# Four preactivation convolution layers on one core: load semaphore split four ways, streamed read issued from ScalarE, VectorE program written out over the images

## The reference

```python
# layer 0: y = leaky(einsum('bchw,oc->bohw', x, W2) + b), slope 0.1
#          (y - min) / (max - min + 1e-8), min and max per image and channel
# layer 1: rfft2, a complex 3x3 convolution over the spectrum, + bias, irfft2
# layer 2: x quantized by the largest |x| of the WHOLE batch, int8 3x3 conv, scale, bias
# layer 3: circular 3x3 convolution (written with FFTs in the reference)
x = x + _L0_conv_ref(_gn(x), ...)
x = x + _L1_conv_ref(_gn(x), ...)
x = x + _L2_conv_ref(_gn(x), ...)
x = x + _L3_conv_ref(_gn(x), ...)
```

## Time and profile before

| | |
|---|---|
| median of 3 runs | 7022.31 us (7016.27 to 7039.35) |
| the profiled execution | 7036.58 us, its span 7033.7 us |
| busy in the span | TensorE 82%, VectorE 71%, ScalarE 64%, GpSimd 39% |
| mean granted TensorE clock | 0.942 |
| DMA | 959.36 MB, mean 136 GB/s |
| issued from SP | 42.4% of the 16 DMA engines' span |
| issued from ScalarE | 6.2% |
| phase 1 | up to 4900 us |
| streamed reads | 224 of 512 KB |
| loads into X in phase 1 from the input | 448 of 256 KB |

### The profile page before, as it was taken

One profiled execution on the slowest core, in us unless ns is written; L12 is line 12 of the kernel. 1 busy time (PEld: TensorE's weight loads), 2 busy tenths in 40 slices (PEclk: granted clock), 3 DMA queues, 4 the chain that ended last, 5 costly groups with the idle time before them and its releaser, 6 DMA issues. The chain is left out here.

```text
span 7033.7 us, 203784 instructions
## 1 busy us (share of the span) xinstructions
PE 5742.6 (82%) x64138; PEld 3678.9 (52%) x64138; DVE 5000.3 (71%) x9849; ACT 4504.5 (64%) x8680; POOL 2727.5 (39%) x4633
## 2 busy tenths in 40 slices
PE   0259968968987896996897898897698898899889
PEld 0037747746764773774675676675243343343334
DVE  7857776767777776776776787787776676676674
ACT  0367656647656665665664654654887778778776
POOL 2145545536545554554553654654011111111112
PEclk9979989989998998998998999998899999999999
DMA  6315524542551551453354154254476676676665
GB/s 179 114 48 164 166 79 121 165 128 74 167 156 48 158 166 58 144 167 103 99 163 145 51 142 125 56 143 113 87 205 169 168 197 167 169 193 180 167 181 132
DMA packets 535643, 959.36 MB, mean 136 GB/s; under 512 B 121946, under 2 KB 126682, under 8 KB 532826
## 3 DMA queue, kind: packets, MB, share of 16 engines
q1 hardware_dynamic: 471898, 815.99, 42.4%
q10 hardware_dynamic: 63104, 134.23, 6.2%
HBM read 560.66 MB, written 287.60 MB: 121 GB/s over the span
## 5 line engine op out<-in xcount | busy, mean ns | idle before, releaser
L868 PE MATMUL pM<-gw,xh 64*128 64x256 f16 (+1 forms) x24960 | 1153.4, 247 | 205.3 <-DMA back<-c_back 205.0
L1570 PE MATMUL pC<-xs,taps 128*128 128x512 f16 x4608 | 1093.8, 382 | 106.4 <-DMA xhalo<-xs 101.3
L868 PEld LDWEIGHTS pM<-gw,xh 64*128 64x128 f16 x24960 | 981.7, 96 | 352.9 <-DMA back<-c_back 230.7
L604 POOL TENSOR_TENSOR X<-X,zo 128x256 f32 (+1 forms) x512 | 370.9, 724 | 1494.5 <-DVE X L1015 1494.5
L1570 PEld LDWEIGHTS pC<-xs,taps 128*128 128x128 f16 x4608 | 448.6, 98 | 669.5 <-DVE xs L1619 90.2
L1466 POOL TENSOR_TENSOR xn<-xn,one_col 128x1 f32<-128x1 f32 x520 | 170.7, 328 | 1402.0 <-ACT xn L1500 1402.0
L775 PE MATMUL pM<-X,mix0s 64*64 64x512 f32 x2304 | 529.9, 632 | 183.9 <-DVE X L987 108.7
L589 POOL TENSOR_TENSOR X<-X,rl 128x512 f32 x384 | 478.0, 1274 | 517.3 <-ACT rl L635 517.0
L1486 ACT ACTIVATE scaled<-X,qbias,qscale 128x512 f32 (+1 forms) x512 | 411.1, 804 | 356.3 <-DMA X<-after_layer 289.4
L1015 DVE SCALAR_TENSOR_TENSOR X<-pZ,X 128x512 f32 (+1 forms) x512 | 353.9, 691 | 376.2 <-ACT zo L664 374.4
L1508 ACT ACTIVATE xs<-xn 128x1028 f16<-128x1028 f32 x520 | 545.7, 1049 | 88.3 <-POOL xn L1467 87.3
(11 more groups left out here) (236 smaller groups left out, 13835.1 us busy)
## 6 DMA issues: line engine op xcount, KB each, us to landing
gw<-row_weights SPq DMA_DIRECT2D x520, 288.0 KB, 3.6
after_layer<-X SPq DMA_DIRECT2D x512, 256.0 KB
out_dram<-result SPq DMA_DIRECT2D x512, 256.0 KB
stage<-in_x_dram SPq DMA_DIRECT2D x224, 512.0 KB
X<-in_x_dram SPq DMA_DIRECT2D x448, 256.0 KB
X<-after_layer ACTq DMA_DIRECT2D x224, 512.0 KB, 5.8
xhalo<-xs SPq DMA_DIRECT2D x504, 96.4 KB, 3.6
qhalo<-q SPq DMA_DIRECT2D x496, 96.2 KB, 4.0
```

What stands on the lines that cost most here:

```text
L604: nc.gpsimd.tensor_tensor(X[:, j, 0], X[:, j, 0], zo[:, k], ALU.add)
L868: nc.tensor.matmul(pY[:, r, col:col + nd * P], row(xh, r)[:, k, p, ri, off:off + P], weights(r, q_, d, nd, ri), start=ri == 0 and off == 1 ...
L1570: nc.tensor.matmul(bank, taps3[:, d, wh], xs[:, h, own, d:d + W], start=d == 0 and n == 0, stop=False)
```

## The change

The single semaphore `loaded` becomes four, one for each tile number modulo 4; `stream` moves from SP's program to ScalarE's; VectorE's loop over the images is unrolled in the program text.

```diff
-            loaded = sem("loaded", p1)
+            loaded_0 = sem("loaded_0", p1)
+            loaded = [sem(f"loaded{k}", p1) for k in range(4)]
...
                     def load(b, j, k, n, more):
-                        wait_alone(sp, loaded, (b * J + j) * 16, passed)
+                        wait_alone(sp, loaded[k], (b * (J // 4) + n) * 16, passed)
...
-                            sp.dma_start(Xf[:, j], image_view(b)[:, :, j]).then_inc(loaded, 16)
+                            sp.dma_start(Xf[:, j], image_view(b)[:, :, j]).then_inc(loaded[k], 16)
...
-                    def turn(b, n, k, g, more, last):
-                        if not last and k % 2 == 0 and (4 <= n < J if isinstance(n, int) else True):
-                            stream(b + 2, g * 2 + k // 2, k // 2)
+                    def turn(b, n, k, g, more):
...
                         for u in range(4):
                             row_weights(b, u, u)
-                        if not last:
-                            for p in range(2):
-                                stream(b + 2, p, p)
...
-                    for p in range(2):
-                        stream(1, p, p, True)
-                    with sp.Fori(1, J // 4) as g:
-                        for s in range(2):
-                            stream(1, g * 2 + s, s)
...
                 def _(act):
+                    def stream(b, p, s, first=False):
+                        if not first:
+                            wait_alone(act, sum_x_done, (b - 1) * PAIRS + p, passed)
+                        act.dma_start(stage[:, s].rearrange("p (t w) -> p t w", t=2),
+                                     image_view(b)[:, :, bass.ds(2 * p, 2)]).then_inc(staged[s], 16)
...
-                    def step(b, i, k4, on, more=False, g=None):
+                    def step(b, i, k4, on, more=False, g=None, ahead=False):
                         k, o = k4 % 2, (k4 + 1) % 2
+                        if ahead and k == 0:
+                            stream(b + 2, i // 2 - 2 if isinstance(i, int) else g * 2 + k4 // 2 - 2, k4 // 2)
                         if on(4):
                             odd_out(b, i - 4, k)
...
-                    with act.Fori(0, J // 4) as g:
+                    for p in range(2):
+                        stream(1, p, p, True)
+                    with act.Fori(0, J // 4 - 1) as g:
                         for s in range(2):
                             next_squares(0, g * 2 + s, s, g)
                             next_sums(0, g * 2 + s, s)
+                            stream(1, g * 2 + s + 2, s)
+                    for p in range(PAIRS - 2, PAIRS):
+                        next_squares(0, p, p % 2, J // 4 - 1)
+                        next_sums(0, p, p % 2)
...
                     def next_pair(b, p):
-                        wait_alone(pe, loaded, ((b + 1) * J + 2 * p + 2) * 16, passed)
+                        for t in range(2):
+                            wait_alone(pe, loaded[(2 * p + t) % 4], ((b + 1) * (J // 4) + p // 2 + 1) * 16, passed)
...
-                    with dve.Fori(0, B) as b:
+                    for b in range(B):
```

More of the change, by code:

```diff
@@ L297, in _ @@
                             if c:
[L298 to L302, removed]
+                                act.wait_ge(loaded_0, 16 * c)
+                            act.dma_start(Xf[:, 4 * c:4 * c + 4], image_view(0)[:, :, 4 * c:4 * c + 4]).then_inc(loaded_0, 16)
+                        act.wait_ge(loaded_0, 16 * (J // 4))
+                        for k in range(4):
+                            act.sem_inc(loaded[k], 16 * (J // 4))
                     @block.vector
@@ L524, in load @@
                         if more:
[L525 removed]
+                            sp.dma_start(Xf[:, j], image_view(b)[:, :, j]).then_inc(loaded[k], 16)
                         else:
[L528 to L535, removed]
[L537 to L540 removed]
+                            sp.dma_start(Xf[:, j], x2s[0].rearrange("(j s) c w -> (s c) j w", s=BANDS)[:, j]).then_inc(loaded[k], 16)
+                    def turn(b, n, k, g, more):
                         if not isinstance(n, int) or n + 4 <= J:
@@ L546, in turn, with image @@
                             load(b + 1, n - 4, k, g - 1, more)
-                    def image(b, more, last):
+                    def image(b, more):
                         for u in range(4):
                             row_weights(b, u, u)
-                        if not last:
-                            for p in range(2):
-                                stream(b + 2, p, p)
                         for n in range(4):
-                            turn(b, n, n, 0, more, last)
+                            turn(b, n, n, 0, more)
                         with sp.Fori(1, J // 4 - 1) as g:
                             for k in range(4):
-                                turn(b, g * 4 + k, k, g, more, last)
+                                turn(b, g * 4 + k, k, g, more)
                         for n in range(J - 4, J + 4):
-                            turn(b, n, n % 4, n // 4, more, last)
-                    for p in range(2):
-                        stream(1, p, p, True)
-                    with sp.Fori(1, J // 4) as g:
-                        for s in range(2):
-                            stream(1, g * 2 + s, s)
+                            turn(b, n, n % 4, n // 4, more)
                     if B > 2:
                         with sp.Fori(0, B - 2) as b:
-                            image(b, True, False)
+                            image(b, True)
                     if B > 1:
-                        image(B - 2, True, True)
-                    image(B - 1, False, True)
+                        image(B - 2, True)
+                    image(B - 1, False)
                     for k in range(4):
                         sp.wait_ge(stored[k], 16 * (B * J // 4 + 1))
-                    sp.wait_ge(loaded, (B + 1) * J * 16)
+                    for k in range(4):
+                        sp.wait_ge(loaded[k], (B + 1) * (J // 4) * 16)
                 @block.gpsimd
@@ L747, in image @@
                         for i in range(8):
-                            step(b, i, i % 4, lambda n, i=i: 0 <= i - n < ITEMS, more and i >= 6)
+                            step(b, i, i % 4, lambda n, i=i: 0 <= i - n < ITEMS, more and i >= 6, None, more and i >= 4)
                         with act.Fori(2, J // 4 - 1) as g:
                             for k in range(4):
-                                step(b, g * 4 + k, k, lambda n: True, more, g)
+                                step(b, g * 4 + k, k, lambda n: True, more, g, more)
                         for i in range(J - 4, J + 6):
-                            step(b, i, i % 4, lambda n, i=i: 0 <= i - n < ITEMS, more and i < J + 6)
+                            step(b, i, i % 4, lambda n, i=i: 0 <= i - n < ITEMS, more and i < J + 6, None, more and i < J + 4)
                     if B > 2:
@@ L1055, in _ @@
                     dve.wait_ge(pads_ready, 1)
-                    dve.wait_ge(loaded, J * 16)
+                    for k in range(4):
+                        dve.wait_ge(loaded[k], (J // 4) * 16)
                     link = Chain(links[0])
```

## The result

| | before | after |
|---|---|---|
| median | 7021.38 us (4 runs, 7016.27 to 7039.35) | 6657.03 us (4 runs, 6645.72 to 6661.95) |
| ratio, with its 95% interval | | 0.9474 (0.9453 to 0.9496) |
| profiled execution, span | 7036.58, 7033.7 | 6661.33, 6659.4 |
| mean granted clock | 0.942 | 0.954 |
| six spectral stages | 2709.7 | 2458.9 |

The change is faster by 5.3%. The forecast was 6669 us, 12 us above the median.

The account below looks back on a forecast made before the run. SP's chain of load, landing, load was taken to bound images 0 to 5. Stages 237.1, tails 112.1 and 6.2, less 2 at the start, make 353.4 us off the median 7022.3: 6668.9 us, range 6630 to 6795.

Parts of the forecast that it names:

- Spectral stages: Images 0 to 5: each stage falls to 412.1 us, from 2709.7 us for six, a gain of 237.1 us.
- The 2 us at the beginning of a stage: Spectral stages of images 0 to 5: 2.0 us over image 6's 408.1, before any load can be late.
- The 2 us kept at the end for a late streamed piece: End of each spectral stage, images 0 to 5: ScalarE still waits for the last streamed piece, 2 us.
- The issue on ScalarE: 192 streamed-read issues ahead of `odd_out`: hidden in idle time, 0 us; 123 us if none is hidden.
- Tails: Ends of images: 20.9 us each, VectorE's gaps gone; gains 112.1 us for six and 6.2 after image 6.
- The start: ScalarE's sums of image 1: 2 us lost waiting for GpSimd's memset; the rest 0, between -20.5 and +10.
- cross-check: Whole kernel: waits for weights 205.0, for loads 119.4 and VectorE's gaps 43.3 add to 367.7 us.
- B: Spectral stages: the transfers, not SP, were the limit; 102 us back, 6771 us; chance 0.13.
- C: Spectral stages: the issue on ScalarE is not hidden; 123 us back, 6792 us; chance 0.09.
- D: Image heads or loads: VectorE's gaps stay, 43 us back, 6712 us, or loads stay serial, 43 as well; chance 0.10.
- F: ScalarE stops for late pieces, slower than before; landings over 12.2 us needed, 7207 us at 15; chance 0.02.
- E: Better: table loads at the start go, 6648 us, or TensorE's clock stays up beyond image 6's; chance 0.05.

Follow-up runs that it names:

- S: The part with four load semaphores in place of one; alone on the kernel before: 6685.3 us, ratio 0.9529.
- e8: Changed kernel with each streamed read issued by ScalarE as four DMAs of 128 KB instead of one of 512 KB; 6747.4 us.
- e12: Kernel before with SP held at the head of each image until VectorE has written that image's scales; 7005.2 us, ratio 0.9964.
- e2: Kernel before with only the streamed read moved from SP to ScalarE; one load semaphore and VectorE's loop kept; 6975.3 us.
- A: The part that moves the streamed read from SP to ScalarE; alone on the kernel before: 6975.3 us, ratio 0.9940.
- e1: Kernel before with only the four load semaphores; streamed read on SP and VectorE's loop kept; 6685.3 us.
- e4: Changed kernel with the streamed read back on SP; four semaphores and VectorE written out stay; 6663.2 us.
- e9: Changed kernel with two load semaphores (tile number modulo 2) instead of four; 6656.8 us.
- e10: Changed kernel with ScalarE's first loop written out and its first two streamed reads issued before the wait for GpSimd's memset; 6635.0 us.
- e7: Changed kernel with each streamed read issued by ScalarE as two DMAs of 256 KB instead of one of 512 KB; 6659.0 us.
- e11: As e10, with a third buffer for the streamed pieces of image 1; 6598.6 us.

## Why the prediction was right, point by point

**The bound.** SP's chain of load, landing, load was named as the bound of images 0 to 5 and the semaphores as what removes it. Shown: S alone brings every stage to 410, all combinations without S stay at 444 or above on average.

**Spectral stages:** forecast 412.1 each and 237.1 us in all, measured 409.8 and 250.8. The 2 us at the beginning of a stage are still there (the first `odd_out` comes 27.4 us after the mark, 25.5 in image 6 of before), but they do not belong to images 0 to 5: in image 7 of before it comes at 27.3. What differs is TensorE's granted clock. From the mark to about the first `odd_out` it is 0.83 in image 6 and 0.74 in image 7 of the kernel before, that is, image 7 begins with more time at 1.2 GHz:

```profile
3954.00:3980.00 26.00, 19.62 (x295) 16.40 (x295) 12.18 (x24) 13.09 (x26) 16.83 (x28) 0.83 0.05 14
...
4474.30:4501.00 26.70, 20.79 (x288) 16.99 (x289) 11.26 (x22) 12.81 (x25) 16.83 (x28) 0.74 0.05 14
```

So the sum's 410.1 was right with the reason for its 2.0 unseen. The 2 us kept at the end for a late streamed piece were the mis-sized term: between 450 and 4500 us ScalarE does not wait for a single piece. The term was 6 x (412.1 - 409.8) = 13.8 us too much.

**The issue on ScalarE:** forecast 0 between 0 and 123. Measured 0, and with twice the issues still 0. The reason given, 1.03 us of idle time ahead of `odd_out` and a start under `yt`, holds for one issue and for two (1.45 us) but is not the limit: e8 goes far over it and pays 0.23 us per piece.

**The move's worth.** The sum treated the move and the semaphores as one term, so it did not say which carries it. The reading that SP's removed work helps was too kind: alone it is worth 41 us of the six stages, beside S nothing.

**Tails:** forecast 20.9 each, measured 122.9 / 6 = 20.5; 112.1 and 6.2 us forecast, 114.6 and 6.7 measured. The gaps went entirely. The Trainium skill's statement in "Runtime: NRT & Kernel Launch", section "Instruction fetch mechanics", that a taken branch out of the fetched window forces a fetch, agrees with the traces: without the jump there is no gap and no instruction packet beside it (e12's section). What the sum had not seen is that more than half of their 43.3 us (22.5 in e12, 23.3 in e2) was made by the two streamed reads in SP's burst and would have gone with A and nearly all with S; beside S the written-out loop is worth 6685.3 - 6663.2 = 22.1 us (e1 against e4).

**The start:** forecast 2 us lost. TensorE's wait for `leaky` is 49.3 us in both profiles, so 0 in all. The 2 us were lost: the first read is issued 0.4 us after the memset's end (238.6), where it was issued 1.6 before. The stretch from that issue to the first `leaky` is 2.7 us shorter, 174.6 instead of 177.3, one table load of 1.28 us among them, and makes up for it. The phase itself began 7 us later in this execution (`scale0_ready` at 362.8 instead of 356.0); in the profiles of e1 to e9 it lies anywhere between 354.6 and 362.1, so no part of the change is shown behind it. The lower bound of that term, 20.5 us for the table loads, is near what e10 collected, together with its earlier issue.

**Nothing else:** phase 2 is 6.8 us shorter in the profile after. Its programs are the same, and among the twelve experiments it takes between 2132 and 2153 us; no part of the change is shown behind it.

**Together:** 250.8 + 114.6 + 6.7 from stages and tails, 6.8 from phase 2, 3.9 from mixing stages (1.6 of it image 0's, 1.0 image 6's), less 6.8 for the later start and 1.7 for image 6's own stage, is 374.3, the difference of the two spans. By medians it is 364.4 against the forecast's 353.4. That the later start and the shorter phase 2 cancel is luck. So is the cross-check's near hit at 367.7: the weights' waits stand for the stages, 205.0 against 250.8 measured, and the loads' waits and the gaps for the tails, 162.7 against 121.3; only the sum agrees.

**The rivals.** B (the transfers were the limit) fell with e1, C (the issue on ScalarE's path) with e7, D with the tails. F needed landings above 12 us; over the whole span the profile after has two groups of waits of ScalarE for a piece, both of the start:

```profile
ACT L671 <- DMA stage<-in_x_dram: 293.1, 15, 247.3
...
ACT unused_x L671 <- DMA stage<-in_x_dram: 6.9, 4, 3.3
```

E's first half came true in e10, outside the change. Its second half, a clock above image 6's, did not: 0.98 in every stage of the profile after, 0.99 in image 6 of before.

## What to carry to other kernels

When the queue engine waits for a landing before it issues the next transfer of a stream, every other transfer in its program order waits too; count that wait per slot (here two slots are enough) before moving transfers to another queue, which alone was worth an eighth as much. Look for stretches of the same trace in which one ingredient is missing, as images 6 and 7 were here, but ask what else is missing there: image 6 had neither the read's issue nor its bytes. A part's worth depends on the others: the written-out loop gave 55 us alone and 22 beside the semaphores.

## What the runs showed that was not expected

- A jump back to the head of VectorE's long loop stalls it 0.6 to 1.2 plus about 2.1 us, and up to 6.4 plus 2.6 when two 512 KB reads were issued 3 to 4.5 us before it begins; eight weight DMAs alone do not stretch it. An 8 KB instruction packet stands in the trace at each of these stalls and at none of the heads without the jump.
- ScalarE's hardware loop over Square and Identity loads an activation table once per iteration, 1.28 us; written out, the same sums load it once (e10, e11).
- ScalarE can spend 3 us at the head of every second step on issuing DMAs, in a pipeline that TensorE fills to 97%, for 0.23 us.
- A spectral stage that nothing holds up takes one of two values, 408.0 to 408.6 or 409.8 to 410.7 us, in kernels with and without S. In the profiles of the kernel before, e7 and e9 every stage of the lower value begins with less time at the 1.2 GHz level. In the kernel before most of the difference is paid back ahead of it: image 6's mixing stage takes 86.2 us and image 7's 85.1. What sets the clock's fall was not tried.
